# Mixture-of-experts slots: 38 slots of one expert each, or 31 such slots and 4 whose two halves have experts of their own

## The reference

```python
x = x + _L0_ffn_ref(_layernorm(x), shared_gate, shared_up, shared_down, routed_gate, ...)

def _expert(x, wg, wu, wd):
    return silu(x @ wg) * (x @ wu) @ wd              # 256 -> 704 -> 256
shared_out = _expert(x, shared_gate, shared_up, shared_down)
probs = sigmoid(x @ Wr * routing_bias)               # 7 routed experts
scores, idx = top_k(probs, 2); scores = scores / scores.sum(-1)
weights[token, idx] = scores
for e in range(7):
    combined = combined + _expert(xf, routed_gate[e], ...) * weights[:, e:e + 1]
return shared_out + combined
```

## Time and profile before

| | |
|---|---|
| median of 3 runs | 1606.47 us |
| the profiled execution | 1609.45 us |
| its span | 1607.6 us |
| PE busy | 1451.6 us, 90% |
| DVE busy | 1097.7 us, 68% |
| ACT busy | 855.7 us, 53% |
| POOL busy | 775.0 us, 48% |
| mean granted clock of PE | 0.966 of full speed |

### The profile page before, as it was taken

The page is one execution under the profiler, slowest core; times in us unless marked ns, Lnnn a source line. Parts: engine busy times, 40 slices in busy tenths (PEclk is TensorE's granted clock), DMA queues, the critical chain, the costliest instruction groups (busy, mean ns, idle before and its releaser), DMA issues.

```text
span 1607.6 us, 43463 instructions
## 1 busy us (share of the span) xinstructions
PE 1451.6 (90%) x17222; PEld 1090.2 (68%) x17222; DVE 1097.7 (68%) x1975; ACT 855.7 (53%) x1850; POOL 775.0 (48%) x689
## 2 busy tenths in 40 slices
PE   3788998999999999999998766999999999999987
PEld 2455665666666766666666555878888888888865
DVE  2786889888888888888888469774444444444457
ACT  1566876777778777777777322452323222222321
POOL 1575777767676767776776300003333333333210
PEclk9898999999999999999999678999999999999998
DMA  5577776777777776767784332643322222222182
GB/s 135 110 161 132 141 135 129 138 143 130 144 129 148 137 149 135 147 129 139 128 154 84 70 99 73 172 138 67 70 69 73 70 71 70 73 71 72 50 265 73
DMA packets 468338, 185.98 MB, mean 116 GB/s; under 512 B 418065, under 2 KB 456289, under 8 KB 468145
## 3 DMA queue, kind: packets, MB, share of 16 engines
q1 hardware_dynamic: 457392, 150.04, 47.2%
q0 software_dynamic: 10752, 33.17, 6.0%
HBM read 62.56 MB, written 18.35 MB: 50 GB/s over the span
## 4 chain that ended last, share of the span: by engine, by line
PE 56%; DVE 23%; ACT 11%; DMA 4%; issue 4%; SPq 2%; POOL 1%; DVEq 0%; POOLq 0%
PE ps L1013 23%; PE ps L1040 11%; PE ps L741 8%; DVE experts L1380 6%; ACT experts L1116 4%; DVE work L1511 4%; PE ps L733 4%; ACT experts L1103 3%; PE ps L758 2%; DVE experts L1468 2%; DMA experts<-experts 2%; PE ps L785 2%; PE ps L728 1%; DVE experts L1419 1%; PE ps L1045 1%
## 5 line engine op out<-in xcount | busy, mean ns | idle before, releaser
L1013 PE MATMUL ps<-work,experts 128*128 128x256 f16 x3564 | 408.3, 276 | 36.9 <-DVE work L1675 13.9
L1013 PEld LDWEIGHTS ps<-work,experts 128*128 (+1 forms) x3564 | 344.8, 99 | 91.3 <-DVE work L1675 14.7
L741 PE MATMUL ps<-experts 128*128 128x512 f16 (+2 forms) x2304 | 364.9, 310 | 30.9 <-DVE work L1524 14.5
L741 PEld LDWEIGHTS ps<-experts 128*128 128x128 f16 x2304 | 198.9, 100 | 174.1 <-DVE work L1524 28.7
L1103 ACT ACTIVATE work<-work 128x768 f16<-128x768 f32 (+1 forms) x140 | 104.4, 745 | 379.0 <-PE ps L1045 245.1
L1116 ACT ACTIVATE experts<-ps,experts 128x256 f32<-128x256 f32 x512 | 203.3, 473 | 74.9 <-DVE experts L1380 74.7
L687 POOL DMA_INDIRECT work<-token_in,work x76 | 73.8, 971 | 317.3 <-DMA work<-work 225.8
L620 POOL TENSOR_TENSOR experts<-experts 128x1024 f16<-128x1024 f32 x96 | 191.8, 1998 | 59.8 <-ACT experts L1103 59.8
L1040 PE MATMUL ps<-experts,work 128*128 (+1 forms) x1620 | 198.3, 276 | 3.7 <-DVE work L1688 3.7
L1040 PEld LDWEIGHTS ps<-experts,work 128*128 128x128 f16 x1620 | 155.5, 99 | 29.5 <-DVE work L1688 4.1
L1380 DVE TENSOR_REDUCE experts<-ps 128x4 f32<-128x1024 f32 x128 | 155.8, 1218 | 11.6 <-PE ps L758 10.5
(11 more groups left out here) (193 smaller groups left out, 2188.8 us busy)
## 6 DMA issues: line engine op xcount, KB each, us to landing
experts<-in_ctx SPq DMA_DIRECT2D x32, 512.0 KB, 5.0
experts<-choice_out POOLq DMA_DIRECT2D x8, 1024.0 KB, 13.1
experts<-in_x SPq DMA_DIRECT2D x32, 128.0 KB, 2.3
token_in<-experts SPq DMA_DIRECT2D x32, 128.0 KB, 2.8
work<-in_L_ffn_routed_gate SPq DMA_DIRECT2D x8, 352.0 KB, 3.1
experts<-experts SPq DMA_TRANSPOSE x160, 4.6
work<-in_L_ffn_routed_up SPq DMA_DIRECT2D x8, 320.0 KB, 4.2
out<-x_all POOLq DMA_DIRECT2D x5, 512.0 KB, 3.3
```

Source lines behind the costliest of these rows:

```text
L741: ins = pe.matmul(bank, lhs[a][k], rhs[b][k], start=(k == 0 and a + b == 0), stop=(last and k == len(lhs[0]) - 1 and a == 1))
L1013: ins = pe.matmul(out, experts_h[:, e, lo:lo + P], e_rows_t[k][:, b * DK + kk, :], start=(kk == 0 and a + b == 0), stop=(kk == DK - 1 and ...
```

## The change

Rows are counted in halves of 128. Each expert's choices are filled up to a multiple of 128 only, which needs `NHALF` = (8192 + 7 * 127) // 128 = 70 halves at the most. An expert's halves go in pairs into slots of one expert; an expert with an odd number has one half left over, and these lie in the last four slots, which are mixed: each of their halves has an expert of its own (where pairs are left over beyond the 31 full slots, they go there too). There are 31 full slots and 4 mixed ones, 35 in all; `NT` becomes 51, `MID` 45.

On PE, `columns` takes a list of experts. With one it issues what it did. With two it issues a block twice, each with 128 rows and its own weights: 12 matmuls of 128 rows in place of 6 of 256. `down` already went by halves, and takes the expert of the half. On DVE the arithmetic of places is longer.

```diff
-NSLOT = (NB * SQ * TOPK + NE * (R - 1)) // R
+NHALF = (NB * SQ * TOPK + NE * (P - 1)) // P
+NMIX = (NE + 1) // 2
+NFULL = NHALF // 2 - NMIX
+NSLOT = NFULL + NMIX
+NEXP = NFULL + 2 * NMIX
...
-        def columns(out, t, k, e, at):
-
-            for kk in range(DK):
-                for a, b in ((0, 0), (0, 1), (1, 0)):
-                    lo = a * EW + 2 * kk * HID + at
-                    ins = pe.matmul(out, experts_h[:, e, lo:lo + P], e_rows_t[k][:, b * DK + kk, :],
-                                    start=(kk == 0 and a + b == 0), stop=(kk == DK - 1 and a == 1))
+        def columns(out, t, k, es, at):
+
+            n = R // len(es)
+            for r, e in enumerate(es):
+                for kk in range(DK):
+                    for a, b in ((0, 0), (0, 1), (1, 0)):
+                        lo = a * EW + 2 * kk * HID + at
+                        ins = pe.matmul(out[:, r * n:(r + 1) * n], experts_h[:, e, lo:lo + P],
+                                        e_rows_t[k][:, b * DK + kk, r * n:(r + 1) * n],
+                                        start=(kk == 0 and a + b == 0), stop=(kk == DK - 1 and a == 1))
             return ins
...
-        def down(t, e):
+        def down(t, es):
...
-                out, rows = ps[:, 7, r * D:(r + 1) * D], slice(r * P, (r + 1) * P)
+                out, rows, e = ps[:, 7, r * D:(r + 1) * D], slice(r * P, (r + 1) * P), es[r % len(es)]
...
-        def expert_of(t):
-            return pe.value_load(tile_e[0:1, t:t + 1], min_val=0, max_val=NE)
-
-        e_before = 0
+        def experts_of(t):
+            j = t - FIRST
+            at = [FIRST + j] if j < NFULL else [FIRST + NFULL + 2 * (j - NFULL) + r for r in range(2)]
+            return [pe.value_load(tile_e[0:1, k:k + 1], min_val=0, max_val=NE) for k in at]
+
+        e_before = SHARED
...
-        link(v.tensor_scalar(r_ni, r_cum[:, NTILE - 1, :], float(R - 1), None, ALU.add))
-        link(v.tensor_scalar(r_ni, r_ni, R.bit_length() - 1, None, ALU.arith_shift_right))
-        link(v.tensor_copy(r_n[:, 0, :], r_ni))
-        link(v.tensor_tensor_scan(r_n[:, 1, :], r_n[:, 0, :], r_n[:, 0, :], 0.0, ALU.add, ALU.bypass))
-        link(v.tensor_tensor(r_n[:, 2, :], r_n[:, 1, :], r_n[:, 0, :], ALU.subtract))
-        link(v.tensor_scalar(r_n[:, 3, :], r_n[:, 2, :], float(R), None, ALU.mult))
+        link(v.tensor_scalar(r_ni, r_cum[:, NTILE - 1, :], float(P - 1), None, ALU.add))
+        link(v.tensor_scalar(r_ni, r_ni, P.bit_length() - 1, None, ALU.arith_shift_right))
+        link(v.tensor_scalar(r_oi, r_ni, 1, None, ALU.bitwise_and))
+        v.tensor_copy(r_halves, r_ni)
+        link(v.tensor_copy(r_odd, r_oi))
+        link(v.tensor_tensor(r_even, r_halves, r_odd, ALU.subtract))
+        v.tensor_scalar(r_limit, r_even, float(P), None, ALU.mult)
+        v.tensor_tensor_scan(r_even_to, r_even, r_even, 0.0, ALU.add, ALU.bypass)
+        link(v.tensor_tensor_scan(r_odd_to, r_odd, r_odd, 0.0, ALU.add, ALU.bypass))
+        v.tensor_scalar(r_base, r_even_to[:, NE - 1:NE], 2.0 * NFULL, None, ALU.max)
+        v.tensor_tensor(r_start, r_even_to, r_even, ALU.subtract)
+        link(v.tensor_tensor(r_jump, r_odd_to, r_odd, ALU.subtract))
+        v.tensor_scalar(r_odd_end, r_odd_to, r_base, None, ALU.add)
+        v.tensor_scalar(r_start, r_start, float(P), None, ALU.mult)
+        link(v.tensor_scalar(r_jump, r_jump, r_base, float(P), ALU.add, ALU.mult))
+        link(v.scalar_tensor_tensor(out=r_jump, in0=r_even_to, scalar=-float(P), in1=r_jump, op0=ALU.mult, op1=ALU.add))
...
-        link(v.tensor_tensor(r_pos, r_pos, bc(r_n[:, 3, :], 1, NTILE), ALU.add))
+        link(v.tensor_tensor(r_eq, r_pos, bc(r_limit, 1, NTILE), ALU.is_ge))
+        v.tensor_tensor(r_pos, r_pos, bc(r_start, 1, NTILE), ALU.add)
+        link(v.tensor_tensor(r_eq, r_eq, bc(r_jump, 1, NTILE), ALU.mult))
+        link(v.tensor_tensor(r_pos, r_pos, r_eq, ALU.add))
```

More of the change, by code:

```diff
@@ L60 @@
                   ("par", 2), ("head4", 4), ("gla", NCH * CH), ("upper", P), ("eps", 1), ("lnscale", 1),
-                  ("one", 1), ("tile", NSLOT), ("desc", NE), ("iota", P), ("rowid", TOPK), ("spare", 2),
+                  ("one", 1), ("tile", NEXP), ("desc", NE), ("iota", P), ("rowid", TOPK), ("spare", 2),
                   ("tnum", NTILE)):
@@ L98, in constants @@
     put("one", np.ones((P, 1)))
-    put("tile", np.arange(NSLOT)[None, :])
+    put("tile", np.concatenate([2 * np.arange(NFULL), 2 * NFULL + np.arange(2 * NMIX)])[None, :])
     put("desc", np.arange(NE, 0, -1)[None, :])
@@ L323, in program @@
     r_m = place3(6 * NTILE).rearrange("p (k t) -> p k t", k=6)
[L324 to L327, removed]
+    r_n = place3(9 * NE).rearrange("p (k e) -> p k e", k=9)
+    r_halves, r_odd, r_even, r_even_to, r_odd_to, r_limit, r_start, r_jump, r_odd_end = (r_n[:, k, :] for k in range(9))
+    r_base = place3(1)
+    r_ni, r_oi = (place3(NE).bitcast(I32) for _ in range(2))
+    r_t = place3(NEXP * NE).rearrange("p (j e) -> p j e", e=NE)
+    r_tf = place3(NEXP)
+    r_to, r_tm = (place3(2 * NMIX) for _ in range(2))
     r_bias = place3(NE)
@@ L1023, in up @@
             for c in blocks_of:
-                ins = columns(ps[:, 1 + c // 2, (c % 2) * R:(c % 2 + 1) * R], t, k, e, c * P)
+                ins = columns(ps[:, 1 + c // 2, (c % 2) * R:(c % 2 + 1) * R], t, k, es, c * P)
             ins.then_inc(S["gate_done"], 1)
@@ L1028, in up @@
                 if c < HT - 1:
-                    ins = columns(ps[:, 4 + c // 2, (c % 2) * R:(c % 2 + 1) * R], t, k, e, HID + HR + c * P)
+                    ins = columns(ps[:, 4 + c // 2, (c % 2) * R:(c % 2 + 1) * R], t, k, es, HID + HR + c * P)
             ins.then_inc(S["up_done"], 1)
-        def down(t, e):
+        def down(t, es):
             wait(pe, S["hid_lo_ready"], t * 2 + 2)
@@ L1068, in _ @@
         for t in range(1, TABLE):
-            tile(t, t % 2, 0, 0)
+            tile(t, t % 2, SHARED, SHARED)
         pe.wait_ge(S["lane_hot_ready"], TOPK)
@@ L1083, in _ @@
         for t in range(TABLE, FIRST):
-            tile(t, t % 2, 0, 0)
+            tile(t, t % 2, SHARED, SHARED)
         pe.wait_ge(S["chunk_lo_ready"], NCHUNK * NE)
-        def expert_of(t):
-            return pe.value_load(tile_e[0:1, t:t + 1], min_val=0, max_val=NE)
-        e_before = 0
+        def experts_of(t):
[3 more added lines that the diff above has]
+        e_before = SHARED
         for t in range(FIRST, MID):
[L1091 to L1094, removed]
+            es = experts_of(t)
+            tile(t, t % 2, es, e_before)
+            e_before = es
+        tile(MID, MID % 2, SHARED, e_before)
         for t in range(MID + 1, NT):
-            tile(t, t % 2, 0, 0)
-        down(NT - 1, 0)
+            tile(t, t % 2, SHARED, SHARED)
+        down(NT - 1, SHARED)
     @block.scalar
@@ L1914, in chunks_of @@
     return range(sum(CHUNKS_AT[:t]), sum(CHUNKS_AT[:t + 1]))
+SHARED = [0]
 BOUND = float(np.exp(60.0) * GK ** -0.5)
@@ L1921 @@
 ROUTE_SELECTED = 3 + 5 * TOPK + 1 + 2
-ROUTE_PARTS = ROUTE_SELECTED + 4 + 2 + NE + 6 + 3 + 2 * TOPK + 5
-ROUTE_HOT = ROUTE_PARTS + 5 + 3 * TOPK
+ROUTE_PARTS = ROUTE_SELECTED + 4 + 2 + NE + 9 + 5 + 2 * TOPK + 5
+ROUTE_HOT = ROUTE_PARTS + 9 + 3 * TOPK
 _SPARE = NCHUNK * (NE - 2)
```

18 lines of the change are left out of this document (12 added, 6 removed).

## The result

| | before | changed |
|---|---|---|
| median, first comparison (8 runs each) | 1606.6 us | 1597.28 us |
| profiled execution | 1609.45 us | 1593.8 us |
| its span | 1607.6 us | 1592.0 us |

The ratio of the changed kernel to the one before is 0.9933, 95% interval [0.9917, 0.9949]: 10.8 us less (8 to 13; the two medians alone differ by 9.3). In two more comparisons it was 0.9901 [0.9868, 0.9935] and 0.9950 [0.9932, 0.9968]. The three together lie around 0.993. The forecast was 13 us less, 1593.5. In one later comparison one of the 12 executions of before took 2067.91 us at a mean granted clock of 0.647; the ratios leave it out.

What follows compares the result with a forecast made beforehand. PE's work bounds the slots, its sequencer the mixed ones; -34.0 (three slots) + 18.0 (mixed slots) + 3.0 (routing) = -13.0 us, 1596.5 from the profiled execution, so median forecast 1593.5 us, own range 1589 to 1599, stated range 1586 to 1601.

Steps and rivals of the forecast that it cites:

- Three slots gone: PE's slots: removing three of 11.33 us each, wholly on the path, saves 34.0 us.
- Four mixed slots: PE's last four slots: bound by its sequencer, 63.3 us in place of 45.3, so +18.0 us.
- a reading: PE's sequencer in a mixed slot: fetching one expert's number takes 0.65 us, two 1.3, with the array idle.
- the first one: First mixed slot: cheaper, 14.7 us, its numbers read while the slot before is still queued.
- The step that decides: PE's sequencer in mixed slots: a register instruction every 0.131 us with its 1.5 matmuls, whatever the matmul's columns.
- Routing: DVE ahead of `hidden(1, 0)`: 18 more instructions, 3.7 us (3.3 to 4.3), passed to PE in full; net +3.0 us.
- The reductions behind it: Behind the added routing arithmetic: two shorter `half_of`, 0.2 us each, and 64 shorter matmuls, about 0.3 us less.
- Two of the signs that I named: Trace signs: clock 1.00 in the mixed slots; PE's idle behind L1683 growing as much as DVE's 3.7 us delay.
- the two with a faster sequencer: Mixed slots: array-bound at 11.5 us each, 1576 us total, chance 0.10; or 14.8 us each, 1589 us, chance 0.05.
- The one with more exposed: Mixed slots: waits and instruction fetches meet an empty queue, 1.5 us a slot more, 1600 us; chance 0.08.
- The slower one: Mixed slots: the array's clock falls, 23.2 us a slot, +16.5 us in all, 1623 us; chance 0.05.
- the silu of the last gates stays covered: Wait within a mixed slot: covered by 24 matmuls, 2.1 us, where 1.3 us were enough before.

Runs made afterwards that it cites:

- 35 slots of one expert: Changed kernel with the last four slots taking one number for both halves, so half their rows get the wrong expert: 1580.4 us, 0.9835 of before.
- constant experts: Changed kernel with fixed experts in the four mixed slots, no readings or register instructions there, results of wrong experts: 1577.32 us, 0.9799 of before.
- mixed slots apart: Changed kernel with each mixed slot followed by one of one expert and numbers read in the slot ahead: 1591.87 us, 0.9908 of before.
- later arithmetic: Changed kernel with the ten DVE instructions on experts' numbers moved from ahead of `hidden(1, 0)` to behind the reading of the row lists: 1593.17 us, 0.9923 of before.

## Why the prediction was right

Point by point, forecast and measured:
- Three slots gone: 34.0; with 35 slots of one expert 34.0.
- Four mixed slots +18.0; measured 63.9 - 45.3 = +18.6. The pieces: the step of the register instruction 0.131, measured 0.13; a reading 0.65, measured 0.65 (1465.0 to 1465.6); a mixed slot 16.2, measured 16.38 and 16.34; the first one 14.7 without the reading of the next, measured 16.13 less 1.36 = 14.8.
- The step that decides: I gave the sequencer's step without a row that isolates it, reasoning that it is the same with one matmul behind it or two. The constant experts show that it was the bound: 17.9 us went with the register instructions and the readings alone.
- Routing +3.7 on DVE, measured 3.4. Instructions without a wait step by 0.08, near the lower bound of 0.07 and not at the 0.12 that I took. The reductions behind it I put at 0.7; the traces at full clock have 124.05 and 123.85 us before and 122.92 after, 1.0. So the term is +2.4 and not +3.0.
- Sum of the terms as measured: -34.0 + 18.6 + 2.4 = -13.0, the forecast to the tenth. That is luck: two errors of 0.6 cancel.
- Two of the signs that I named were off: the clock in the mixed slots was 0.92 and not 1.00, and PE's idle behind L1683 grew by 2.5 us and not by 3.7.

What stands between that and the 12.0 us of the traces (10.8, 8 to 13, in the whole times) is for the most part the first slot's clock, for which I charged nothing. Its 36 matmuls took 2.8, 2.7 and 0 us more than 4.10 in the three traces of the changed kernel, and 0, 0 and 1.7 us more in those of before, 1.3 us more on the mean. Three traces each do not settle that it is the change's doing. What is left is within the scatter.

Of the rivals, the two with a faster sequencer fall with the constant experts. The one with more exposed is near, 0.2 us a slot and not 1.5. The slower one was right in its first half: the clock does fall behind most idles of 1.3 us in the mixed slots. It costs next to nothing. A matmul of 128 rows at the lower clock takes 0.107 us (I had 0.112), the sequencer gives one every 0.087, and what the array loses in those few us it makes up behind, having 0.056 again. The period is the same with the fall and without it, 16.18 and 16.23. The evidence that I cited against it (idle of 1.18 us in the attention stage without a fall) was too thin: it excluded nothing. One statement held only in part: that the silu of the last gates stays covered in a mixed slot. It does where ACT begins it right behind its gates, as in the changed kernel. Where ACT begins it up to 1.6 us later, as with the mixed slots apart, 0.82 us come to light, and I had not reckoned with that.

## What to carry to other kernels

Where addresses come out of registers, count the register instructions per matmul as well as the columns: here one such step is 0.13 us, and a matmul must be worth 0.087 us or more to hide its share. Halving a matmul's rows doubles this time, though the array's stays the same. Before claiming a saving between two traces, cut them into stages and compare each over several executions; a stage that the change doesn't touch moved by 10 us here.

## What the hardware showed that I had not expected

- The register instruction has a duration of 0.046 us in its rows and a step of 0.13; the step, not the duration, is its price, with one matmul behind it or two.
- With register instructions gone, 132 pairs of weight load and matmul of 128 columns went at 0.056 us each, where the Trainium skill (TensorE: Matmul & The Clock Gate, Back-to-back issue gap) gives a sustained 81 ns; here the measurement decides.
- An idle of 1.3 us, followed by matmuls at 0.087 us in place of 0.056, was in most cases enough for the granted clock to fall for a while (0.58 on the mean of 1450 to 1454), while idle of 3.1 to 3.6 us ahead of the first slot cost the clock in some executions and in others not.
- In the mixed slots of two runs (spread apart, and with the later arithmetic) ACT began the silu of the last gates up to 1.6 us later than in those of the other runs, with its gates done. Why is not shown.
